# Causal mask put into PSUM by ScalarE instead of an identity product on TensorE, with the diagonal score units moved

## What is computed

```
mask  = where(triu(ones(S, S), k=1), -inf, 0)          # S = 512
Q, K, V = heads(x @ WQ), heads(x @ WK), heads(x @ WV)  # 16 heads of width 8
score = einsum("bhqd,bhkd->bhqk", Q, K) / sqrt(8)
score = score + mask
score = exp(score - max(score, axis=-1))
score = score / sum(score, axis=-1)
out   = einsum("bhqk,bhkd->bhqd", score, V)
```

## Time and profile before

| | |
|---|---|
| time, median of 3 runs | 627.11 us (626.76 to 627.77) |
| profiled execution: time | 625.26 us |
| profiled execution: span, first to last instruction | 623.5 us |
| busy: PE, DVE, ACT, POOL | 562.9, 406.0, 329.7, 178.5 us |
| mean granted TensorE clock | 0.975 |
| attention's main loops | about 28 to 198 us of the span |
| unit scores (L1735), mask products (L1738) | 160 and 64 matmuls |
| maxima (L1134) | 160, 102.7 us busy |
| exponentials (L724) | 192, 92.2 us busy |

### The profile page before, as it was taken

How to read it: one execution, slowest core, us unless ns; L and a number is a source line. 1 busy time by engine, 2 the same in 40 slices (tenths; PEclk the granted TensorE clock), 3 DMA queues, 4 the chain that set the end, 5 groups by cost and what they waited for, 6 DMA issues and landing times.

```text
span 623.5 us, 9495 instructions
## 1 busy us (share of the span) xinstructions
PE 562.9 (90%) x3421; PEld 440.6 (71%) x3421; DVE 406.0 (65%) x981; ACT 329.7 (53%) x582; POOL 178.5 (29%) x196
## 2 busy tenths in 40 slices
PE   7899999999998389999386979999999999998997
PEld 3566676666764279999364857787878977896876
DVE  6788799889883514544279868855589556852430
ACT  5766675765766216765044346634475256543451
POOL 6123132552634623666430141014101040001100
PEclk9999999999999589999799989999999999999999
DMA  4485631532300444762311000000000000000000
GB/s 138 161 284 184 245 117 38 184 91 67 94 9 15 136 152 145 254 228 72 94 43 30 6 0 2 0 1 1 2 17 1 0 2 18 0 2 1 17 1 17
DMA packets 31966, 44.69 MB, mean 72 GB/s; under 512 B 4272, under 2 KB 18096, under 8 KB 31664
## 3 DMA queue, kind: packets, MB, share of 16 engines
q1 hardware_dynamic: 29328, 39.05, 19.2%
q0 software_dynamic: 2304, 4.74, 2.1%
q10 hardware_dynamic: 288, 0.30, 0.2%
HBM read 25.16 MB, written 18.91 MB: 71 GB/s over the span
## 4 chain that ended last, share of the span: by engine, by line
PE 69%; DVE 12%; ACT 6%; issue 6%; POOL 4%; DMA 2%; DVEq 0%; SPq 0%; ACTq 0%; POOLq 0%
PE ps L2093 7%; PE ps L1735 5%; PE ps L1751 5%; PE ps L2019 5%; PE ps L2115 5%; PE ps L1763 4%; PE ps L2116 4%; PE ps L2196 4%; PE ps L2192 4%; PE ps L2193 4%; PE ps L2119 4%; DVE pm L1134 3%; PE ps L2109 2%; PE ps L1738 2%; POOL xs_dram L581 1%
## 5 line engine op out<-in xcount | busy, mean ns | idle before, releaser
L1134 DVE TENSOR_REDUCE pm<-ps 128x4 f32<-128x512 f32 x160 | 102.7, 686 | 16.7 <-PE ps L1735 9.4
L724 ACT ACTIVATE PT<-ps 128x384 f32<-128x384 f32 (+1 forms) x192 | 92.2, 527 | 31.7 <-PE ps L1751 28.9
L595 POOL TENSOR_SCALAR_AFFINE_SELECT PT<-PT 128x512 f32<-128x512 f32 x64 | 40.1, 639 | 116.0 <-ACT PT L724 115.9
L1735 PE MATMUL ps<-KP,QS 128*128 128x512 f32 x160 | 67.4, 436 | 1.8 <-ACT VR L704 0.7
L1751 PE MATMUL ps<-QM,KP 128*128 128x512 f32 (+3 forms) x256 | 65.2, 328 | 0.4 <-ACT PT L724 0.4
L1751 PEld LDWEIGHTS ps<-QM,KP 128*128 128x128 f32 x256 | 43.0, 189 | 18.1 <-ACT PT L724 10.2
L634 POOL DMA_INDIRECT ytok_dram<-zero,rowS x40 | 42.4, 1059 | 40.0 <-DVE rowS L1420 29.9
L570 POOL TENSOR_TENSOR rstd<-veps,mhalf 128x4 f32<-128x4 f32 x11 | 12.7, 1154 | 110.3 <-DVE veps L1045 109.1
L1534 DVE TENSOR_TENSOR_SCAN zero<-decay,OG 128x512 f32<-128x512 f32 x32 | 41.7, 1304 | 1.1
L1763 PE MATMUL ps<-PT,V 128*32 128x128 f32 (+3 forms) x512 | 41.5, 439 | 0.0
L935 ACT ACTIVATE hF<-ps,cols 128x512 f32<-128x512 f32 x16 | 11.0, 689 | 55.3 <-PE ps L2196 55.3
(11 more groups left out here) (319 smaller groups left out, 1380.8 us busy)
## 6 DMA issues: line engine op xcount, KB each, us to landing
qk_dram<-HL SPq DMA_DIRECT2D x8, 512.0 KB, 4.0
W<-in_eW SPq DMA_DIRECT2D x16, 256.0 KB, 3.5
QS<-qk_dram SPq DMA_DIRECT2D x15, 256.0 KB, 2.7
KP<-qk_dram SPq DMA_DIRECT2D x60, 64.0 KB
xs_dram<-zero SPq DMA_DIRECT2D x4, 645.0 KB, 3.9
XS<-xs_dram SPq DMA_DIRECT2D x8, 322.5 KB, 3.1
qk_dram<-HL SPq DMA_DIRECT2D x8, 256.0 KB, 4.6
ytok_dram<-zero SPq DMA_DIRECT2D x4, 512.0 KB, 4.7
```

Of the source, the lines that this page charges most:

```text
L595: g.affine_select(out=diag, in_=diag, pattern=[[0, 4], [1, P]], compare_op=ALU.is_ge, fill=0.0, base=0, channel_multiplier=-1).then_inc(se ...
L724: act.activation(PT[:, i, a:z], bank[ROWB + n % KEYB][:, 0:z - a], ACT.Exp, scale=float(DK) ** -0.5).then_inc(exp_done, 1)
L1134: v.tensor_reduce(pm[:, t, k, :], bank[n % ROWB].rearrange("p (i n) -> p i n", n=P), AXX, ALU.max).then_inc(row_free[n % ROWB], 1)
L1735: mm = pe.matmul(to, QS[:, G % 2, t * P:(t + 1) * P], KP[:, G % 3, k, :, :].rearrange("p i n -> p (i n)"), start=True, stop=t != k)
```

## The change

`UNITS` is put in another order, so that the diagonal units become numbers 0, 1, 8 and 9. For those of groups 2 to 15 (`SEEDS`, 56 units) the mask product is left out: ScalarE copies `mask4` into the unit's bank (`seed`), after waiting for `row_free`, and the score matmul, which now waits for `seeded`, adds onto what is there (`start` false). Groups 0 and 1 keep their eight mask products. The copies are called **S8, S9, S0, S1** here: in loop w, S8 and S9 are for units 8 and 9 of group w + 1 and stand after E1 and E2; S0 and S1 are for units 0 and 1 of group w + 2 and stand after E6 and E7.

```diff
--- before.py
+++ after.py
@@ -36,7 +36,7 @@
 NKU = 4 * NK
 ROWB = 3
 KEYB = 3
-UNITS = [(1, 0), (1, 1), (2, 0), (2, 1), (0, 0), (2, 2), (3, 0), (3, 1), (3, 2), (3, 3)]
+UNITS = [(0, 0), (1, 1), (1, 0), (2, 0), (2, 1), (3, 0), (3, 1), (3, 2), (2, 2), (3, 3)]
 PTW = 10 * P
 OFF = [sum(SEQ - i * P for i in range(j)) for j in range(TB + 1)]
 N_CONST = 3 * P + 16 + 2 * NT + 8 + E * ST + ST + 3
@@ -82,7 +82,19 @@
         if before >= 0 and g == 0:
             at["turn", before] = len(at)
     return at
+def _seeds():
+
+    at = {}
+    for w in range(NW):
+        if 2 <= w + 1 < NW:
+            for u in (8, 9):
+                at[u, w + 1] = len(at)
+        if w + 2 < NW:
+            for u in (0, 1):
+                at[u, w + 2] = len(at)
+    return at
 RING = _ring()
+SEEDS = _seeds()
 TURNS = _turns()
 EARLY = {1: 4, 2: 2, 3: 2}
 
@@ -319,7 +331,7 @@
         tp_full, tp_free = sem("tp_full"), sem("tp_free")
         ts_full, exp_done, sel_done = sem("ts_full"), sem("exp_done"), sem("sel_done")
         pv_done, v_ready = sem("pv_done"), sem("v_ready")
-        mx_done, qm_done = sem("mx_done"), sem("qm_done")
+        mx_done, seeded = sem("mx_done"), sem("seeded")
         varA, rsA, xnA = sem("varA"), sem("rsA"), sem("xnA")
         og_done, lT = sem("og_done"), sem("lT")
         og_last, lL = sem("og_last"), sem("lL")
@@ -723,6 +735,13 @@
                 act.wait_ge(ts_full, NKU * w + n + 1)
                 act.activation(PT[:, i, a:z], bank[ROWB + n % KEYB][:, 0:z - a], ACT.Exp,
                                scale=float(DK) ** -0.5).then_inc(exp_done, 1)
+            def seed(u, G):
+
+                n = RING[u, G]
+                act.wait_ge(row_free[n % ROWB], n // ROWB)
+                act.activation(bank[n % ROWB], mask4[:, :, :].rearrange("p i n -> p (i n)").bitcast(F32),
+                               ACT.Copy).then_inc(seeded, 1)
+
             def store_sums(w):
 
                 act.wait_ge(pv_done, TB * w + TB)
@@ -804,7 +823,11 @@
                 if b and g == 2:
                     take_turn("turn2", b - 1, xn2T[:, :])
                 exp_unit(w, 1)
+                if (8, w + 1) in SEEDS:
+                    seed(8, w + 1)
                 exp_unit(w, 2)
+                if (9, w + 1) in SEEDS:
+                    seed(9, w + 1)
                 exp_unit(w, 3)
                 if w:
                     store_sums(w - 1)
@@ -821,7 +844,11 @@
                     tail_norm(b - 1, 0)
                     tail_norm(b - 1, 1)
                 exp_unit(w, 6)
+                if (0, w + 2) in SEEDS:
+                    seed(0, w + 2)
                 exp_unit(w, 7)
+                if (1, w + 2) in SEEDS:
+                    seed(1, w + 2)
             exp_unit(NW - 1, 8)
             exp_unit(NW - 1, 9)
             exp_unit(NW - 1, 10)
@@ -1732,9 +1759,13 @@
                     pe.wait_ge(qs_in[G % 2], 16 * ((G + 1) // 2))
                     pe.wait_ge(kp_in[G % 3], 64 * ((G + 2) // 3))
                 t, k = UNITS[u]
+                sown = (u, G) in SEEDS
+                if sown:
+                    pe.wait_ge(seeded, SEEDS[u, G] + 1)
                 mm = pe.matmul(to, QS[:, G % 2, t * P:(t + 1) * P],
-                               KP[:, G % 3, k, :, :].rearrange("p i n -> p (i n)"), start=True, stop=t != k)
-                if t == k:
+                               KP[:, G % 3, k, :, :].rearrange("p i n -> p (i n)"), start=not sown, stop=t != k or sown,
+                               skip_group_check=sown)
+                if t == k and not sown:
                     mm = pe.matmul(to, identr[:, :], mask4[:, :, :].rearrange("p i n -> p (i n)"),
                                    start=False, stop=True)
                 mm.then_inc(rs_full, 1)
```

## The result

The median went from 627.22 us (626.76 to 627.77; four runs now, where the table above has three) to 645.78 us (644.95 to 647.76): +18.6 us, ratio 1.0316, 95% interval 1.0290 to 1.0342. The profiled execution took 646.27 us with a span of 644.5 and a mean granted clock of 0.966 (before: 625.26, 623.5 and 0.975).

What follows compares the result with a forecast made beforehand. TensorE's queue was taken to set the 9.60 us loop, VectorE close behind. Three plain loops +5.0, ten with tail work +10.1 and loop 0 +1.2 gave +16.3 on 627.1: 643.4, rounded to 643.5, range 634 to 650.

Steps and rivals of the forecast that it cites:

- S0 behind E6: From unit 6's exponential on ScalarE to VectorE's first maximum, waiting for unit 0's copy: 0.41 becomes 1.63, +1.22 us a loop.
- S8 ahead of R8: Unit 8's score matmul, just ahead of the value products, waits for its copy and one more hand-over: +0.65 us a loop.
- S1 and S9 at nothing: Copies for units 1 and 9 on ScalarE finish before anything needs them: no cost.
- The mask behind R9: Removed mask product after unit 9's score matmul, between value products and unit 6's exponential: -0.20 us a loop, ends 0 and -0.23.
- The copy at 0.60: Each 128x512 copy from SBUF to PSUM on ScalarE takes 0.60 us, with 0.49 and 0.69 as ends.
- The new order at nothing: Reordering the units leaves the count of maxima and the QS and KP loads unchanged: no cost.
- The ten loops with tail work: Attention loops that also carry tail steps: 110.81 us before, about 120.9 after, +10.1 us.
- Loop 0: First attention loop pays only the wait for unit 0's copy: +1.2 us.
- Faster: Rival: the copies hide and TensorE's queue keeps its own rate, saving 12.9 us, 614 us; chance 0.06.
- Only the first wait counts: Rival: the wait for unit 8's copy is absorbed, 8.5 us of the sum fall away, 635 us; chance 0.08.
- The clock: Rival: TensorE's new gaps lower its granted clock, adding 53 us, about 697 us and more; chance 0.04.
- TensorE's busy share under 80%: Sign expected in the profile after: TensorE busy under 80% of loops without tail work, at a clock of 1.00.

Runs made afterwards that it cites:

- fourth experiment: The kernel after's new order of units alone, with all 64 mask products and no copies; 627.54 us, ratio 1.0031 to the kernel before.

## Why the prediction was right

Forecast 643.5, measured 645.78, in the range of 634 to 650. By its steps, the plain loop:

- **S0 behind E6**, forecast 0.41 -> 1.63: E6 at 59.33, M0 at 60.96, 1.63. By the timelines S0 starts 0.39 after E6 (I had 0.38), R0's load follows S0's start by 60.43 - 59.72 = 0.71 (0.64), and M0 follows the load by 0.53 (0.61): two small misses that cancel. Taken back alone it gives 1.22 a loop. The largest term, exact in its sum.
- **S8 ahead of R8**, forecast +0.65: from M0 to V 55.06 - 49.53 = 5.53, before 4.40 + 0.50 = 4.90, so +0.63.
- **S1 and S9 at nothing**: they stand in no chain of the kernel after that is shown here, and S9's removal moved nothing that can be told from the spread.
- **The mask behind R9**, forecast -0.20: V to E6 takes 59.33 - 55.06 = 4.27, before 4.29, so -0.02. This is the one term of the plain loop that was mis-sized. I had named the store of the sums as what the turn behind K5 waits for, and took 0.03 off for it; that much the chain shows (57.27), since the store ends at 56.55 + 0.60 = 57.15, just ahead of the turn's load at 57.27. What I had left out: the four transposes of that turn take 0.63 instead of 0.44 when they start from a wait and not behind other work. Rows 7 had a hint of that: the same kind of turn, just after a wait for ScalarE, takes 0.66.
- **The copy at 0.60**: 0.600, mean of 56.
- **The new order at nothing**: right for this change, but not of the order by itself. The order alone puts two mask products on the plain path (+0.45 a loop, fourth experiment); the copies take these very products out again, so neither shows after.

The sum, 5.53 + 4.27 + 1.63 = 11.43, is 0.16 above the forecast 11.27, of which the mask behind R9 is 0.18.

**The ten loops with tail work** were forecast at 120.9 and took 123.6. Ten times 0.16 is 1.6 of the 2.7. The rest lies in single loops, where I had judged whether a tail step is on the new cycle. In one of the three loops with the residual add, the one from 135.88, the residual add and the maxima behind it lead up to S8 (chain of waits):

```profile
139.05 0.69 DVE X L1197
139.74 0.50 DVE pm L1161
...
140.25 0.69 DVE pm L1161
...
140.97 0.61 ACT ps L742
```

From M0 to S8 there are 5.09 instead of the plain loop's 4.31: 0.78, where I had 0.61. In the loop from 148.10, which I had counted as a plain one, V comes only at 154.04, 5.94 after M0 instead of 5.53, and the chain shows why: the turned rows and the logits of the router stand in TensorE's queue ahead of R8. S8 is done before R8's turn comes there, so the 0.65 that I gave S8 in this loop and its like wasn't paid: the logits took its place and cost more.

```profile
150.64 0.54 PE ps L1836 x4
...
152.34 0.91 PE ps L1842 x8
...
154.04 1.43 PE ps L1794 x24
```

So there are two small misses besides the mask behind R9: the residual add was on the path, as forecast, but longer, and the logits were taken to be off the new path and are on it.

**Loop 0**, forecast +1.2, took 10.76 - 9.54 = +1.22. Not foreseen: +0.41 ahead of the first M0 (27.34 instead of 26.93). Unit 0 is now a diagonal one and its mask product, which the first groups keep, stands ahead of that M0; but in the six experiments with the same start that M0 comes at 26.92 to 27.33, so how much of the 0.41 is the product's can't be told from what differs between executions. The end of the attention gives 0.8 of it all back, which I hadn't foreseen either. That the total is only 2.3 too low is in part this luck.

**The rivals.** "Faster" was rightly a matter of S0's place in the queue: with S0 ahead of E6, and V ahead of R8, the copies do hide. "Only the first wait counts" fell: R8 waits for its copy in every plain loop and in eight of the ten with tail work. "The clock" fell: the granted clock is 1.00 through the attention in both kernels, with TensorE idle 1.10 and 1.28 us in each loop. The passage of the Trainium skill that I had weighed against it (TensorE: Matmul & The Clock Gate, section "A second HAM failure mode: psum-queue depth-cycling") isn't borne out at these gaps. One of the marks named ahead, TensorE's busy share under 80%, was wrong: it is 9.59 / 11.43 = 84%. I had taken four products off at 0.23 each, which leaves 8.68 busy. But 0.18 came back in the turn of the sums (the 0.63 above), and from M0 to S8, where TensorE keeps VectorE's pace, it is still busy 4.24 of 4.31 with fewer products: the records of the unit scores there are longer, up to 0.50 where they had been 0.39 to 0.45.

## What to carry to other kernels

Taking work off the busiest engine gains nothing if the engine must then wait, in its in-order queue, for the one that got the work: price the wait, not the work, and look at what stands ahead of the new work in its own queue. Put the handed-over work as early as its buffer allows, and put something independent between the producer's release and the consumer on the waiting engine; here the same 56 copies cost 18.6 us in one place and gained 7.5 in another. A cost found in one kind of loop isn't that of all loops: the order of units cost 0.45 in a plain loop and 0.05 on the mean of those with tail work.

## What was not expected of the hardware

A ScalarE copy of 128x512 fp32 from SBUF to PSUM took 0.600, against 0.599 from PSUM to SBUF and 0.621 from SBUF to SBUF with a rounding to fp32r; without the rounding it was 0.623 (three copies of the kernel before). The Trainium skill (ScalarE: Activation LUTs, section "ACT is a hardware spline evaluator") calls PSUM the faster destination; here that is 0.02 at most, and nothing that a plan could rest on.

From the start of a copy to the start of the matmul that waits for it there are 54.58 - 53.84 = 0.74 for S8 and 60.46 - 59.72 = 0.74 for S0. For the turn that waits for a ScalarE copy in the kernel before it was 77.08 - 76.43 = 0.65: there the hand-over is 0.04, here 0.14. What makes the difference wasn't tried.

The four transposes of the turn of the sums took 0.63 in a plain loop where they began from a wait (the kernel after, the runs with S0 and S1 early and with products for units 0 and 1), and 0.44 where they were queued behind other matmuls (the kernel before and the other five runs). Why wasn't tried.
